# A Mamba-2 block between two feed-forward layers on one core: the skip path moved up on VectorE, the out projection as products of rounded halves that GpSimd makes, and the masked product whole on VectorE

## The reference, cut to what matters

```python
H, P, N, CHUNK = 64, 64, 128, 32        # D_INNER = 4096, D_MODEL = 256
proj = hidden_states @ in_proj_w        # gate | x,B,C | dt
x, B, C = silu(causal_conv4(xBC) + conv_b)
dt  = softplus(dt + dt_bias);  cum = cumsum(dt * -exp(A_log)) in a chunk
Y_diag = ((C @ B.T) * exp(cum_i - cum_j) * mask * dt_j) @ x
states = scan over chunks of (B * exp(cum_end - cum) * dt).T @ x
Y_off  = (C @ previous state) * exp(cum)
hidden = (Y_diag + Y_off + D_param * x) * silu(gate)
hidden = hidden * rsqrt(mean(hidden**2) + EPS) * norm_w
return hidden @ out_proj_w
```

## Time and profile before

| what | value |
|---|---|
| median of 3 runs | 1499.91 us (1498.86 to 1500.24) |
| the profiled execution | 1502.24 us |
| its span in the trace | 1500.5 us |
| mean granted clock of TensorE | 0.966 of full speed |
| one group of 16 slots in the loop's middle | 129.76 to 129.78 us |
| busy in such a group: PE, DVE, ACT, POOL | 128.1, 113.0, 113.5, 75.5 us |

### The profile page before, as it was taken

The page is one execution under the profiler, slowest core; times in us unless marked ns, Lnnn a source line. Parts: engine busy times, 40 slices in busy tenths (PEclk is TensorE's granted clock), DMA queues, the critical chain, the costliest instruction groups (busy, mean ns, idle before and its releaser), DMA issues. The chain is left out here.

```text
span 1500.5 us, 26270 instructions
## 1 busy us (share of the span) xinstructions
PE 1385.1 (92%) x8704; PEld 1088.5 (73%) x8704; DVE 1119.6 (75%) x2675; ACT 1038.7 (69%) x2133; POOL 637.2 (42%) x639
## 2 busy tenths in 40 slices
PE   4889977768999999999999999999999999987998
PEld 4777766556777777777777777777777777764887
DVE  6853444675888888888888888888888888886433
ACT  1124333576898888889888888988888898871332
POOL 1013211023555565656556555655655565561000
PEclk9999989888999999999999999999999999996999
DMA  5220000224445554344454534555543554334000
GB/s 125 71 88 25 15 15 14 68 45 95 114 96 112 125 106 121 98 107 109 109 128 106 110 100 106 117 110 121 114 104 92 119 121 107 98 86 182 15 14 28
DMA packets 102080, 136.37 MB, mean 91 GB/s; under 512 B 27744, under 2 KB 49856, under 8 KB 101824
## 3 DMA queue, kind: packets, MB, share of 16 engines
q1 hardware_dynamic: 99840, 132.67, 37.0%
q10 hardware_dynamic: 2112, 2.10, 0.4%
HBM read 124.76 MB, written 9.96 MB: 90 GB/s over the span
## 5 line engine op out<-in xcount | busy, mean ns | idle before, releaser
L1008 POOL TENSOR_TENSOR hid<-hid,sg 128x512 f32<-128x512 f32 x128 | 209.1, 1634 | 328.2 <-DVE hid L1277 328.2
L845 ACT ACTIVATE M<-cum_row,cum_table 128x128 f32<-128x128 f32 x1024 | 311.9, 389 | 0.0
L1215 DVE SCALAR_TENSOR_TENSOR xs<-psum,conv_w_sb,xs 128x509 f32<-128x509 f32 (+2 forms) x384 | 285.1, 742 | 0.4
L1611 PE MATMUL psum<-hid,wo 128*128 128x512 f32 x512 | 243.1, 597 | 9.4 <-ACT eT L756 9.2
L989 POOL TENSOR_TENSOR M<-M,CB 128x512 f32<-128x512 f32 x128 | 164.3, 1284 | 115.6 <-ACT M L853 115.6
L1269 DVE TENSOR_TENSOR psum<-psum,e_row 128x512 f32<-128x512 f32 x128 | 89.5, 700 | 145.4 <-PE psum L1584 145.4
L997 POOL TENSOR_TENSOR squares<-squares,sq 128x512 f32<-128x512 f32 x124 | 162.3, 1309 | 2.7 <-ACT sq L822 2.7
L1611 PEld LDWEIGHTS psum<-hid,wo 128*128 128x128 f32 x512 | 96.2, 189 | 84.4 <-issue 72.7
L1596 PE MATMUL psum<-M,xdt 128*64 128x128 f32 x2048 | 140.1, 279 | 0.9 <-DVE psum L1269 0.9
L1570 PE MATMUL psum<-xend,B_tok 128*128 128x128 f32 x1024 | 137.6, 278 | 0.0
L853 ACT ACTIVATE M<-M 128x1024 f32<-128x1024 f32 x128 | 134.5, 1050 | 0.5
(11 more groups left out here) (202 smaller groups left out, 3081.6 us busy)
## 6 DMA issues: line engine op xcount, KB each, us to landing
cum_row<-cum_scratch SPq DMA_DIRECT2D x256, 256.0 KB, 4.5
e_row<-e_scratch SPq DMA_DIRECT2D x256, 128.0 KB, 3.5
xw_raw<-L_attn_in_proj_w_dram SPq DMA_DIRECT2D x32, 128.0 KB, 3.1
wo_raw<-L_attn_out_proj_w_dram SPq DMA_DIRECT2D x32, 128.0 KB, 3.2
gw_raw<-L_attn_in_proj_w_dram SPq DMA_DIRECT2D x16, 256.0 KB, 6.7
x_res<-_attn_hidden_states_dram ACTq DMA_DIRECT2D x4, 512.0 KB, 9.9
x_scratch<-x_res SPq DMA_DIRECT2D x4, 512.0 KB, 2.6
x_res<-x_scratch SPq DMA_DIRECT2D x1, 2048.0 KB, 7.7
```

Of the source, the lines that this page charges most:

```text
L845: last = nc.scalar.activation(M[:, v % 3, h, c * CH:(c + 1) * CH], cum_row[:, v % 2, h, c * CH:(c + 1) * CH], ACT.Relu, bias=scalar_of(CUM ...
L1008: nc.gpsimd.tensor_tensor(hid[:, v % 2, :], hid[:, v % 2, :], sg[:, v % 8, :], ALU.mult).then_inc(hid_done, 1)
L1215: nc.vector.scalar_tensor_tensor(xs[:, v % 8, shift:], psum[:, X_BANK + v % 2, 0:TT - shift], tap_of(v, step), xs[:, v % 8, shift:], ALU.m ...
L1611: last = nc.tensor.matmul(psum[:, OUT_BANK + m, :], wo[:, j, m * P:(m + 1) * P], hid[:, v % 2, :], start=(j == 0), stop=(j == GP - 1))
```

## The change

It has these parts in the loop.

1. `skip_path` stands on VectorE between the second and the third tap of the convolution, ahead of the third piece of the scan. It waits for `hid_lo_done` of two slots before where it waited for `out_done`.
2. The out projection uses `split_matmul`: six fp32r matmuls of 512 columns where there were four f32 pieces. GpSimd makes the halves of `hid` in every slot (`split_hid`: a cast, L982, and a subtraction, L985), and those of `wo`. `hid_lo` is one buffer, so its subtraction waits for the out projection of the slot before.
3. GpSimd makes the upper halves of the weights too (`split_x`, `split_g`, `split_wo`, the last with a multiplication by `norm_w`); in the loop ScalarE makes none.
4. `masked` does both heads in one instruction of 1024 elements on VectorE; `masked_second` goes from GpSimd.
5. For room, `e_row` and `xend` have one buffer each and `xdt` two; `gw_raw` is half as large. `load_e` is issued for s+3 and waits for `scale_off` of s+2, the slot just before it.
6. In the first tile the state is zero: `off` and `scale_off` leave the first chunk out, and the scan's first piece is a copy.

The weights' loads and splits stand at other steps (`X_SLOTS`, `G_SLOTS`, `u >= 13`), and in the stage before the loop at other ticks. The diff, cut to that:

```diff
-    e_row = sb("e_row", [P, 2, TT], F32)
-    xdt = sb("xdt", [P, 3, CPT, 2, HP], F32)
-    xend = sb("xend", [P, 2, CPT, 2, HP], F32)
+    e_row = sb("e_row", [P, TT], F32)
+    xdt = sb("xdt", [P, 2, CPT, 2, HP], F32)
+    xend = sb("xend", [P, CPT, 2, HP], F32)
+    hid_hi = sb("hid_hi", [P, 2, TT], F32R)
+    hid_lo = sb("hid_lo", [P, TT], F32R)
...
+    X_SLOTS = (5, 7, 8, 10)
+    G_SLOTS = (6, 9)
...
             def load_e(v):
-                sp.wait_ge(off_scaled, nth(v - 2))
+                sp.wait_ge(off_scaled, nth(v - 1))
...
-                if alive(s + 4):
-                    load_e(s + 4)
+                if alive(s + 3):
+                    load_e(s + 3)
...
         def _(act):
...
-                if g < GROUPS - 1 and u in (6, 8):
-                    split_g_hi(2 * (g + 1) + u // 2 - 3)
-                if g < GROUPS - 1 and 6 <= u < 6 + GP:
-                    split_x_hi((g + 1) * GP + u - 6)
-                if g < GROUPS - 1 and u >= 13:
-                    scale_wo((g + 1) * GP + u - 13)
...
         def _(pool):
...
-            def masked_second(v):
-                nc.gpsimd.tensor_tensor(M[:, v % 3, 1, :], M[:, v % 3, 1, :], cb, ALU.mult).then_inc(M2_done, 1)
+            def split_hid(v):
+                pool.wait_ge(hid_done, nth(v))
+                pool.wait_ge(out_done, nth(v - 2))
+                nc.gpsimd.tensor_copy(hid_hi[:, v % 2, :], hid[:, v % 2, :]).then_inc(hid_hi_done, 1)
+                pool.wait_ge(hid_hi_done, nth(v))
+                pool.wait_ge(out_done, nth(v - 1))
+                nc.gpsimd.tensor_tensor(hid_lo[:], hid[:, v % 2, :], hid_hi[:, v % 2, :].bitcast(F32),
+                                        ALU.subtract).then_inc(hid_lo_done, 1)
+
+            def split_x(p):
+                nc.gpsimd.tensor_copy(xw_hi[:, :, cols], xw_raw[:, p % 2]).then_inc(xw_hi_done, 1)
+                split_x_lo(p)
+
+            def split_wo(p):
+                nc.gpsimd.tensor_tensor(wo_raw[:, p % 2, :], wo_raw[:, p % 2, :], norm_sb[:, p:p + 1].to_broadcast([P, D]),
+                                        ALU.mult).then_inc(wo_done, 1)
+                nc.gpsimd.tensor_copy(wo_hi[:, p % GP, :], wo_raw[:, p % 2, :]).then_inc(wo_hi_done, 1)
+                split_wo_lo(p)
...
             for s in range(-8, ALL):
-                if alive(s + 2):
-                    masked_second(s + 2)
...
                 if alive(s + 1):
                     gate(s + 1)
+                    split_hid(s + 1)
...
+                if u in X_SLOTS:
+                    split_x((g + 1) * GP + X_SLOTS.index(u))
+                if u in G_SLOTS:
+                    split_g(2 * (g + 1) + G_SLOTS.index(u))
+                if u >= 13:
+                    split_wo((g + 1) * GP + u - 13)
...
         def _(dve):
...
-                nc.vector.tensor_tensor(M[:, v % 3, 0, :], M[:, v % 3, 0, :], cb, ALU.mult).then_inc(M_done, 1)
+                nc.vector.tensor_tensor(M[:, v % 3], M[:, v % 3], cb, ALU.mult).then_inc(M_done, 1)
...
             def skip_path(v):
-                dve.wait_ge(out_done, nth(v - 2))
+                dve.wait_ge(hid_lo_done, nth(v - 2))
...
                     conv_tap(s + 7, 1)
                 if alive(s + 2):
                     scan(s + 2, 1)
+                if alive(s + 1):
+                    skip_path(s + 1)
                 if alive(s + 7):
                     conv_tap(s + 7, 2)
...
-                if alive(s + 1):
-                    skip_path(s + 1)
...
         def _(pe):
...
             def out_proj(v):
-                pe.wait_ge(hid_done, nth(v))
-                pe.wait_ge(wo_done, pair_of(v) + 1)
+                pe.wait_ge(hid_hi_done, nth(v))
+                pe.wait_ge(hid_lo_done, nth(v))
+                pe.wait_ge(wo_lo_done, pair_of(v) + 1)
...
-                    last = nc.tensor.matmul(psum[:, OUT_BANK + m, :], wo[:, j, m * P:(m + 1) * P], hid[:, v % 2, :],
-                                            start=(j == 0), stop=(j == GP - 1))
+                    last = split_matmul(nc, psum[:, OUT_BANK + m, :], wo_hi[:, j, cols], wo_lo[:, j, cols],
+                                        hid_hi[:, v % 2, :], hid_lo[:], start=(j == 0), stop=(j == GP - 1))
```

More of the change, by code:

```diff
@@ L401, in macaron @@
     wo_raw = sb("wo_raw", [P, 2, D], F32)
-    wo = sb("wo", [P, GP, D], F32)
+    under, sbu = scope()
+    w_bc_raw = sbu("w_bc_raw", [P, KT, 2 * N], F32)
+    w_dt_raw = sbu("w_dt_raw", [P, KT, H], F32)
+    under.close()
+    wo_hi = sb("wo_hi", [P, GP, D], F32R)
+    wo_lo = sb("wo_lo", [P, GP, D], F32R)
     under, sb = scope()
@@ new lines, in sum_halos @@
+            def sum_halos(v):
+                t, pairs, n = v // GP % NT, slice(pair_of(v), pair_of(v) + GP), sums_before(v)
+                pool.wait_ge(halo_in, GP * n)
+                pool.wait_ge(conv_done, nth(v - 5))
+                for tap in range(TAPS - 1):
+                    w_tap = conv_w_sb[:, pairs, tap:tap + 1].to_broadcast([P, GP, TAPS - 1 - tap])
+                    nc.gpsimd.tensor_tensor(halo_prod[:, tap, :, 0:TAPS - 1 - tap], halo[:, t % 2, :, tap:], w_tap,
+                                            ALU.mult).then_inc(halo_step, 1)
+                pool.wait_ge(halo_step, 5 * n - 2)
+                nc.gpsimd.tensor_tensor(halo_prod[:, 1, :, 0:1], halo_prod[:, 1, :, 0:1], halo_prod[:, 2, :, 0:1],
+                                        ALU.add).then_inc(halo_step, 1)
+                bias = conv_b_sb[:, pairs].unsqueeze(2).to_broadcast([P, GP, TAPS - 1])
+                nc.gpsimd.tensor_tensor(halo_prod[:, 0], halo_prod[:, 0], bias, ALU.add).then_inc(halo_step, 1)
+                pool.wait_ge(halo_step, 5 * n)
+                nc.gpsimd.tensor_copy(halo_sum[:, t % 2, :, 2], halo_prod[:, 0, :, 2])
+                nc.gpsimd.tensor_tensor(halo_sum[:, t % 2, :, 0:2], halo_prod[:, 0, :, 0:2], halo_prod[:, 1, :, 0:2],
+                                        ALU.add).then_inc(halo_done, 1)
@@ new lines, in split_wo_lo, with hid_to_lo @@
+            def split_wo_lo(p):
+                pool.wait_ge(wo_hi_done, p + 1)
+                if p >= GP:
+                    pool.wait_ge(out_done, nth(last_of(p - GP)))
+                nc.gpsimd.tensor_tensor(wo_lo[:, p % GP, :], wo_raw[:, p % 2, :], wo_hi[:, p % GP, :].bitcast(F32),
+                                        ALU.subtract).then_inc(wo_lo_done, 1)
+            def hid_to_lo(v):
+                pool.wait_ge(hid_hi_done, nth(v))
+                pool.wait_ge(sq_done, nth(v))
+                nc.gpsimd.tensor_tensor(hid_lo[:, v % 2, :], hid[:, v % 2, :], hid_hi[:, v % 2, :].bitcast(F32),
+                                        ALU.subtract).then_inc(hid_lo_done, 1)
@@ L1259, in scan @@
                     else:
[L1260 removed]
+                        before = carry[:, t % 2, j, h, :]
                     after = carry[:, (t + 1) % 2, j, h, :] if c == CPT - 1 else inner[:, v % 2, c, h, :]
@@ L1570, in states @@
                     last = nc.tensor.matmul(psum[:, ST_BANK, c * P:(c + 1) * P], B_tok[:, t * CPT + c, :],
-                                            xend[:, v % 2, c].rearrange("p h q -> p (h q)"), start=True, stop=True)
+                                            xend[:, c].rearrange("p h q -> p (h q)"), start=True, stop=True)
                 last.then_inc(states_done, 1)
@@ L1577, in off @@
                 pe.wait_ge(v_done, nth(v - 1))
-                for c in range(CPT):
-                    if c > 0:
-                        before = inner[:, v % 2, c - 1]
-                    else:
-                        before = zero_state[:] if t == 0 else carry[:, t % 2, j]
+                first = 1 if t == 0 else 0
+                for c in range(first, CPT):
+                    before = inner[:, v % 2, c - 1] if c > 0 else carry[:, t % 2, j]
                     tok = (t * CPT + c) * CH
@@ L1585, in off @@
                                             before.rearrange("p h q -> p (h q)"), CT[:, tok:tok + CH],
-                                            start=(c == 0), stop=False, skip_group_check=True)
+                                            start=(c == first), stop=False, skip_group_check=True)
                 last.then_inc(off_done, 1)
```

155 lines of the change are left out of this document (79 added, 76 removed).

## The result

The changed kernel takes **1472.78 us** in the median of four runs (1469.96 to 1473.38), the kernel before in the same session 1500.08. The ratio is 0.9814, with a 95% interval of 0.9802 to 0.9826: 27 to 28 us faster. The forecast was 1488.4, 11.5 faster; the time lies in the stated range, but the gain is 2.4 times the one forecast.

A forecast was written before the change was run, and what follows sets the result against it. TensorE bound the loop, with VectorE's free time gone after the change. Per group 119.4 + 4.0 + 4.4 = 127.8 us against 129.77; over seven and a half groups, less end losses, 1488.4 us, range 1456 to 1518 (main case 1476 to 1497).

The forecast's parts named there:

- TensorE's floor: Projections and out projection on TensorE: without waits, TensorE alone would do a group of 16 slots in 121.1 us.
- The skip path: VectorE's skip path, moved earlier: all 2.7 us a group of TensorE's waits go if nothing takes their place.
- VectorE's work: VectorE in the loop: 113.05 us a group becomes 119.4 with the whole mask product, so its free time is gone.
- The port: VectorE's mask product waits for GpSimd instructions reading SBUF: 0.25 us a slot, 4.0 a group, bounds 0 and 10.2.
- One buffer of `e_row`: Loads for the scaling of Y: rows land 1.1 us late four times a group, 4.4 us; bounds 0 and 8.
- 0 if ScalarE keeps up: Lower bound of the charge for late `e_row` loads, as ScalarE loses 0.3 us a slot of splits.
- Idle time of VectorE taken as nothing: VectorE in the loop: its free time was held to be gone, so the group's sum had no idle term.
- TensorE's wait for `gw_lo`: Gate weights split on GpSimd at u = 9, just before `proj_g`: 0 to 1 us a group, 0 taken.
- The end of the loop: Last eight slots, GpSimd's chain longest: +1.6 us; last out projection waits for a cast and a subtraction: +1.9.
- That waits do not come: Rival: mask product finds the port free, `e_row` lands in time, groups about 122.5 us, 1449 us; chance 0.15.
- That the port makes it slower: Rival: mask product waits 0.5 us or more in the average slot on GpSimd, giving 1519 us; chance 0.25.
- the rival on the other side: The slower outcome: mask product's port waits outweigh the gains, 1519 us, or 1535 at the bound; chance 0.25.

The follow-up runs named there:

- the kernel with GpSimd relieved: Changed kernel without GpSimd's sum of squares and, after the first slot, without the `hid_lo` subtraction: 1447.50 us, ratio 0.9640.
- with the skip path late: Changed kernel with the skip path back in its old place on VectorE, behind the last scan piece: 1508.29 us, ratio 1.0044.
- run 1: Not a follow-up run: the words are part of "run 1% shorter", said of some steps of the changed kernel, which takes 1472.78 us.

## Why the prediction was right and wrong, point by point

- **TensorE's floor, 121.1 us a group: right.** The out projection takes 1.38 us (1.40), and the kernel with GpSimd relieved comes within 1.1 us of the floor.
- **The skip path, 2.7 us a group: right**, shown alone: 129.77 to 127.15.
- **VectorE's work, 119.4: nearly.** Busy 121.9 less 3.5 of waits inside the mask product is 118.4. The mask product alone takes 1.22 us, as 1.05 ns an element gave.
- **The port, 4.0 us a group: right** in kind and size: 3.5 by the mean; 3.2 went when most of its causes were taken away, `gw_lo`'s 0.8 perhaps among them. The prediction had the gate over when the mask product comes and `hid_lo` still waiting; it is just these two that hold it, the gate in 28 of 96 slots and `hid_lo` in 12.
- **The step that failed is "One buffer of `e_row`", 4.4 us a group.** It measured 0 to 1.4, 0.3 in the mean, by leaving the loads out; the waits that a landing ends are 0.7 in the group shown. The mechanism is real (3.7 us a group with the skip path late), but the landing was mis-sized. I let the second load go out at 970.4 and gave it the longest time to landing of the earlier trace rows, 5.1 us. That time is the first load's:

```profile
L616 SPq DMA_DIRECT2D e_row<-e_scratch x1: 1541/1541/1541, 968.9 to 968.9; - x1
...
DMA to landing us min/median/max: 5.1/5.1/5.1
```

  The second landed 4.4 us after its issue, at 974.8, so in the step that I read the rows were 0.2 us late against 974.6 and not 0.9: 0.7 too much, four times a group. I also let a faster loop leave ScalarE later. It came earlier: the last `e_row` went out 1.08 us after the scaling before, in the mean of 26 late steps, where I had 2.7, and the rows had landed after 6.4 us where I had 7.8. The bound that I named for this, "0 if ScalarE keeps up", is where the term ended. With the landing read right it would have been 1.6 and the sum 125.0, but that nearness to 125.4 would have been partly luck, since idle time was missing from the sum.
- **Idle time of VectorE taken as nothing: it is 2.3 us a group**, its wait for `off`, which hides some of the other miss. In the sum's own terms the group shown is 118.5 of work, 3.5 for the port, 0.7 for `e_row` and 2.3 idle, 125.0; the forecast had 119.4, 4.0, 4.4 and 0. TensorE's wait for `gw_lo`, which I had bounded by 1 and taken as 0, is 0.8; VectorE's longest wait for `off`, 1.17 us, stands just behind it and is 0.4 to 0.6 in the kernel with GpSimd relieved, so part of the 2.3 is probably its work.
- **The end of the loop: right.** From slot 120 of the loop on, the kernel loses 4 us of what it had gained (32.1 us at the exponentials of slot 120, 1298.96 - 1266.89, and 27.8 at the final sum of squares, 1360.49 - 1332.71); 3.5 were charged.
- **The rivals.** That waits do not come (1449 us) has its image in the kernel without squares and `hid_lo`, 1447.5. That the port makes it slower needed 0.37 us a slot, with `e_row` at 4.4; it was 0.22. In the order with the skip path late the changed parts lose against the kernel before (1.0044), so the rival on the other side was one instruction's place away.
- **The range of the forecast does not follow from its sum.** Waits of 0.1 and 0.3 us a slot give groups of 125.4 and 128.6, which is 1470 and 1494 us, where 1476 to 1497 was written. The measured 1472.8 lies outside the written range and inside the one that follows; the group of 125.4 came about in another way, with 0.22 a slot and almost nothing for `e_row`.

Over 7.5 groups the 2.4 us between 127.8 and 125.4 are 18 us, the whole distance between the forecast span (1489.0) and the measured one (1471.7). What the shorter out projection, the first tile's shorter work and the smaller buffers bring or cost each by itself has no run.

## What to carry to other kernels

Where one engine sets the pace in most steps and another makes it wait in a few, look first for the one instruction whose place causes those waits: here it was worth 24 us, against 4 for shorter matmuls and all that was moved to make them possible (12 in the loop's groups, less what both ends gave back). When work goes from the slowest engine to others, price the others' free time too. When you price a late load, pair each issue with its own landing and look at several of the steps, not at one: here the longest landing set behind the latest issue made a wait of 0.2 us into 0.9. Whether two engines collide on a port is a matter of where in the step their instructions fall: a quarter less load on GpSimd only moved the collisions from the gate to `hid_lo`, while taking out `hid_lo` too gave 22 us more.

## What the runs showed of the hardware

- A cast of 512 f32 elements to fp32r on GpSimd takes 0.61 us, half of a subtraction with two inputs (1.28), and it too is held up by VectorE's product of two SBUF operands. The changed kernel's timeline has this near the loop's end, on GpSimd and on VectorE:

```profile
1319.38 1.28 POOL L1060 TENSOR_TENSOR hid<-hid,sg 128x512 f32<-128x512 f32 x1 [0.35 <-DVE hid L1340]
1320.73 1.49 POOL L982 CAST hid_hi<-hid 128x512 fp32r<-128x512 f32 x1
```

```profile
1319.61 2.14 DVE L1299 TENSOR_TENSOR M<-M,CB 128x1024 f32<-128x1024 f32 x1
```

  The mask product starts 0.23 us after the gate and ends 1.09 us after the gate does (1321.75 against 1320.66), a little under its whole length; the cast, which started before that end, ends 0.47 after it. The Trainium skill ("SBUF — State Buffer", Who interferes with whom) gives the exclusion for GpSimd instructions that read SBUF; the trace agrees. The rows add an order: VectorE's waiting instruction went ahead of GpSimd's next one, so that one wait is at most the rest of one GpSimd instruction. It is so in every one of the 57 mask products of the changed kernel that took over 1.30 us: each ended 1.07 to 1.09 us after the GpSimd instruction that it had started behind, and the longest took 2.14. For the product of 512 elements in the kernel before that time is 0.55 us, all seven times.
- Some steps of the changed kernel run 1% shorter on two engines: the third tap takes 0.73 us in place of 0.74 on VectorE in 17 of 119 slots, and the matmuls of 512 columns follow each other after 0.227 us ((992.03 - 990.67) / 6) in place of 0.230 ((999.64 - 998.26) / 6) on TensorE. I cannot tell from these runs whether the clock or the profile's time base moves.
- With `e_row` not loaded, the DMA engines moved 81 GB/s in place of 115 and the mean pace changed by 0.3 us a group, `e_row`'s own waits included: the DMA load itself costs no more than that here.
